# Recurrence and top-4 mixture of experts on one core: no dummy matmuls between the recurrence's steps, b2 as one rounded pass over stacked gates, gate transposes behind the down product

## The reference

```python
# x: (32 sequences, 32 steps, 128), h0 = cond: (32, 128)
xw = x @ Wx + b
h[t] = tanh(xw[:, t] + h[t-1] @ Wh)            # 32 steps, one after the other
# mixture of experts over the 1024 tokens h, 16 experts, 4 chosen
xn = h * rsqrt(mean(h * h) + 1e-5) * norm_scale
vals, idx = top_k(xn @ wg + bg, 4)
gate_full = one_hot(idx) @ softmax(vals)       # (1024, 16)
hh = xn @ w1[e] + b1[e]                        # 128 -> 2 x 128, for every expert
a, b = min(hh[::2], 7), clip(hh[1::2], -7, 7)
s = a * sigmoid(1.702 * a) * (b + 1)
y = s @ w2[e] + b2[e]
out = x + h + sum over e of gate_full[:, e] * y[e]
```

## Time and profile before

| | |
|---|---|
| three runs | 109.14, 109.22, 110.36 us; median 109.22 |
| profiled execution | 110.22 us, span of its instructions 108.4 us |
| PE busy | 102.9 us (95%), 562 matmuls |
| weight loads busy | 87.0 us (80%) |
| DVE, ACT, POOL busy | 64.6 (60%), 60.8 (56%), 63.8 us (59%) |
| chain that ended last, by engine | PE 79%, DVE 9%, ACT 5%, DMA 2% |

### The profile page before, as it was taken

One profiled execution on the slowest core, in us unless ns is written; L12 is line 12 of the kernel. 1 busy time (PEld: TensorE's weight loads), 2 busy tenths in 40 slices (PEclk: granted clock), 3 DMA queues, 4 the chain that ended last, 5 costly groups with the idle time before them and its releaser, 6 DMA issues.

```text
span 108.4 us, 1718 instructions
## 1 busy us (share of the span) xinstructions
PE 102.9 (95%) x562; PEld 87.0 (80%) x562; DVE 64.6 (60%) x173; ACT 60.8 (56%) x139; POOL 63.8 (59%) x76
## 2 busy tenths in 40 slices
PE   7899999999999999999999969999999999999980
PEld 2557689988899999999989958886888888888760
DVE  0101367876818976399747996578266656666730
ACT  5144826899646486767716645665364566645400
POOL 3004348987791996449980799896444466545400
PEclk9999999999999999999999999999999999999999
DMA  2997930007930002991058814991000000000012
GB/s 77 235 335 266 398 113 0 0 6 234 390 159 3 0 0 74 296 379 39 12 165 246 308 60 116 336 361 59 6 0 0 0 3 0 0 0 0 0 48 48
DMA packets 4936, 12.94 MB, mean 119 GB/s; under 512 B 752, under 2 KB 1728, under 8 KB 4928
## 3 DMA queue, kind: packets, MB, share of 16 engines
q1 hardware_dynamic: 4704, 12.67, 34.7%
q10 hardware_dynamic: 224, 0.17, 0.6%
HBM read 12.25 MB, written 0.59 MB: 118 GB/s over the span
## 4 chain that ended last, share of the span: by engine, by line
PE 79%; DVE 9%; ACT 5%; DMA 2%; issue 1%; DVEq 0%
PE psA L774 19%; PE psB L774 17%; PE psY L804 10%; PE psR L804 5%; PE psR L722 5%; PE psM L804 5%; PE psY L722 2%; DMA wx_x_sb<-in_wx_x 2%; PE psA L751 2%; PE psM L729 2%; PE psR L714 2%; ACT psA L483 2%; PE psR L816 2%; ACT psA L492 2%; PE psM L816 2%; DVE lin L667 1%
## 5 line engine op out<-in xcount | busy, mean ns | idle before, releaser
L406 POOL TENSOR_TENSOR actg<-act,gate_cols 128x512 f32<-128x512 f32 x31 | 39.4, 1279 | 13.7 <-DVE act L682 12.9
L667 DVE TENSOR_SCALAR lin<-psB,one_b1b 128x256 f32<-128x256 f32 (+1 forms) x48 | 26.0, 569 | 23.3 <-PE psB L774 23.3
L483 ACT ACTIVATE psA<-psA,lim_b1a 128x256 f32<-128x256 f32 (+1 forms) x48 | 23.8, 515 | 26.5 <-PE psA L774 26.5
L682 DVE SCALAR_TENSOR_TENSOR act<-lin,psA 128x512 f32<-128x512 f32 x32 | 21.9, 686 | 1.8 <-ACT psA L492 0.5
L492 ACT ACTIVATE psA<-psA,limit_col 128x512 f32<-128x512 f32 x32 | 21.1, 660 | 0.8
L774 PE MATMUL psA<-xn_hi,w_hi 128*128 128x256 f32 (+1 forms) x48 | 20.5, 428 | 0.0
L804 PE MATMUL psY<-actg,w_sb 128*128 128x256 f32 x64 | 17.1, 389 | 0.0
L774 PE MATMUL psB<-xn_hi,w_hi 128*128 128x256 f32 (+1 forms) x48 | 16.0, 332 | 0.0
L774 PE MATMUL psA<-xn_hi,w_lo 128*128 128x256 f32 (+1 forms) x48 | 15.8, 328 | 0.0
L774 PE MATMUL psB<-xn_lo,w_hi 128*128 128x256 f32 (+1 forms) x48 | 15.6, 325 | 0.0
L774 PE MATMUL psB<-xn_hi,w_lo 128*128 128x256 f32 (+1 forms) x48 | 15.5, 323 | 0.0
(11 more groups left out here) (82 smaller groups left out, 136.0 us busy)
## 6 DMA issues: line engine op xcount, KB each, us to landing
gate_cols<-gate_rows SPq DMA_DIRECT2D x16, 512.0 KB, 6.0
w_sb<-in_w SPq DMA_DIRECT2D x4, 512.0 KB, 8.0
w_sb<-in_w SPq DMA_DIRECT2D x4, 256.0 KB, 9.3
out<-yT SPq DMA_DIRECT2D x3, 128.0 KB, 1.7
wx_x_sb<-in_wx_x SPq DMA_DIRECT2D x1, 320.0 KB, 6.0
wx_x_sb<-in_wx_x SPq DMA_DIRECT2D x2, 128.0 KB, 2.5
small_h<-in_small ACTq DMA_DIRECT2D x1, 105.0 KB, 2.7
gate_rows<-gT SPq DMA_DIRECT2D x4, 16.0 KB, 1.4
```

Of the source, the lines that this page charges most:

```text
L406: nc.gpsimd.tensor_tensor(by_pair(actg[:, u % SUM_DEPTH, w]), by_pair(act[:, u % ACT_DEPTH, w]), gate_block(u, w), ALU.mult).then_inc(actg ...
L483: last = nc.scalar.activation(psA[u % 2][:, o], psA[u % 2][:, o], ACT.Relu, scale=-1.0, bias=lim_b1a[:, e0 + k:e0 + k + 1])
L667: last = nc.vector.tensor_scalar(lin[:, v % 2, o], psB[v % 2][:, o], one_b1b[:, e0 + k:e0 + k + 1], LIMIT + 1.0, ALU.add, ALU.min)
L682: nc.vector.scalar_tensor_tensor(act[:, v % ACT_DEPTH, 0:w], lin[:, v % 2, 0:w], 1.0 - LIMIT, psA[v % 2][:, 0:w], ALU.max, ALU.mult).then_ ...
```

## The change

1. PE's head: the ten dummy matmuls between steps and the one behind them are gone. The raw logits of tile 0 come after step 6, those of tile 1 behind the sums of tile 1; `x_wx(3, 2)` becomes `x_wx(3, 1)` ahead of `lay_rstd(1)` and `x_wx(4, 1)` behind it.
2. b2 comes three times stacked (48 x 128). DVE rounds it to fp32r and replaces the third copy by what rounding left (`b2_parts`, at v = 1). The gates are laid out as [rounded, rest, rounded, zeros, exact], 80 columns (`gates_split`, two more DVE instructions a pair, and one more POOL memset at the start), so one rounded product with 48 rows adds high x high, low x high and high x low. The transposes are 80 x 128; ACT copies the exact part (gT) and then the stacked part (gS, fp32r). `down` waits for gS.
3. From v = 4 on the transposes stand behind `down(v - 4)`.
4. The last chunk's accumulators are 384 and 128 columns wide (psR, psM) in place of 256 and 256; the last product waits for both of DVE's pieces, and the last addition and store are 128 columns wide.

```diff
@@ gates_scale
-                nc.vector.tensor_tensor(
+                mark(nc.vector.tensor_tensor(
                     gates[:, ts, :], gate_sum[:, ts, :],
                     inv[:, ts].rearrange("p (j o) -> p j o", o=1).to_broadcast([P, 2, E]),
-                    ALU.mult).then_inc(scale_done, 1)
+                    ALU.mult))
+
+            def gates_split(q):
+
+                settled()
+                ts = slice(2 * q, 2 * q + 2)
+                high = gates_w[:, ts, 0:4 * E].rearrange("p j (a b e) -> p j a b e", a=2, b=2)[:, :, :, 0, :]
+                mark(nc.vector.tensor_copy(high.bitcast(F32R), gates[:, ts, :].rearrange("p j (a e) -> p j a e", a=1)
+                                           .to_broadcast([P, 2, 2, E])))
+                settled()
+                nc.vector.tensor_tensor(gates_w[:, ts, E:2 * E], gates[:, ts, :], gates_w[:, ts, 0:E],
+                                        ALU.subtract).then_inc(scale_done, 1)
@@ copy_gates
-                nc.scalar.activation(gT[:, q * PW:(q + 1) * PW], psX[0:E, 0:PW], ACT.Copy).then_inc(gT_ready, 1)
+                qc = slice(q * PW, (q + 1) * PW)
+                nc.scalar.activation(gT[:, qc], psX[4 * E:5 * E, 0:PW], ACT.Copy).then_inc(gT_ready, 1)
+                nc.scalar.activation(gS[:, qc], psX[0:3 * E, 0:PW], ACT.Copy).then_inc(gS_ready, 1)
@@ vector
+            def b2_parts():
+
+                dve.wait_ge(b2_loaded, 16)
+                mark(nc.vector.tensor_copy(b2_w[:, :], b2_sb[:, :]))
+                settled()
+                low = slice(2 * E, 3 * E)
+                nc.vector.tensor_tensor(b2_w[low, :], b2_sb[low, :], b2_w[low, :].bitcast(F32),
+                                        ALU.subtract).then_inc(b2_ready, 1)
@@ transpose_gates
-                    last = nc.tensor.transpose(psX[0:E, k * P:(k + 1) * P], gates[:, j, :], ident[:, :])
+                    last = nc.tensor.transpose(psX[0:5 * E, k * P:(k + 1) * P], gates_w[:, j, :], ident[:, :])
@@ down
-                    pe.wait_ge(gT_ready, first_pair(c + 1))
+                    pe.wait_ge(gS_ready, first_pair(c + 1))
                     for o, y in y_parts(c):
-                        nc.tensor.matmul(y, b2_sb[:, :], gT[:, cols(c)][:, o], start=True, stop=False)
+                        nc.tensor.matmul(y, b2_w[:, :], gS[:, cols(c)][:, o], start=True, stop=False)
@@ head of the tensor program
                 step(t)
-                if t in (0, 1, 2, TL, TL + 2):
-                    keep_warm(2)
-                elif t == 3:
+                if t == 3:
                     x_wx(1, 1)
                 elif t == TL + 1:
                     pe.wait_ge(consts_ready, 1)
                     sums(0).then_inc(m_mm, 1)
-                else:
+                elif t == TL + 2:
+                    pe.wait_ge(wg_ready, 1)
+                    raw_logits(range(0, 1), psB[0])
+                elif t == HEAD - 1:
                     lay_rstd(0)
                     x_wx(2, 1)
-            keep_warm(1)
+            sums(1).then_inc(m_mm, 1)
+            raw_logits(range(1, 2), psB[0]).then_inc(raw_mm, 1)
             pe.wait_ge(step_done, HEAD)
-            sums(1).then_inc(m_mm, 1)
-            pe.wait_ge(wg_ready, 1)
-            raw_logits(pair_tiles(0), psB[0]).then_inc(raw_mm, 1)
+            x_wx(3, 1)
             lay_rstd(1)
-            x_wx(3, 2)
+            x_wx(4, 1, start=False)
@@ loop over the units
-                for q in at(GATES_T, v):
-                    transpose_gates(q)
+                if v < LAG:
+                    for q in at(GATES_T, v):
+                        transpose_gates(q)
                 for q in at(STATS, v):
                     sums(pair_group(q))
                     raw_logits(pair_tiles(q), psM).then_inc(m_mm, 1)
                 if v >= LAG:
                     down(v - LAG)
+                    for q in at(GATES_T, v):
+                        transpose_gates(q)
@@ the last chunk
-                return [(slice(k * PW, (k + 1) * PW), y_end_bank(k)[:, 0:PW]) for k in range(2)]
+                return [y_end(k) for k in range(2)]
@@ down_half
-                    pe.wait_ge(actg_tail, k + 1)
+                    pe.wait_ge(actg_tail, 2)
```

More of the change, by code:

```diff
@@ L92, in adaln_rnn_moe_kernel @@
         bg_sb = sb("bg_sb", [P, E])
-        b2_sb = sb("b2_sb", [E, H])
+        b2_sb = sb("b2_sb", [3 * E, H])
+        b2_w = sb("b2_w", [3 * E, H], F32R)
         w1_sb = sb("w1_sb", [H, E, 2, I])
@@ L128, in adaln_rnn_moe_kernel @@
         gate_sum = sb("gate_sum", [P, NT, E])
-        gates = sb("gates", [P, NT, E])
-        gT = sb("gT", [E, NT * P])
+        gates_w = sb("gates_w", [P, NT, 5 * E])
+        gates = gates_w[:, :, 4 * E:5 * E]
+        gT_all = sb("gT_all", [5 * E, NT * P])
+        gT = gT_all[4 * E:5 * E, :]
+        gS = sb("gS", [3 * E, NT * P], F32R)
         gate_rows = nc.dram_tensor("gate_rows", [NQ, E, PW], F32)
@@ L176, in adaln_rnn_moe_kernel @@
         gT_ready = sem("gT_ready")
+        gS_ready = sem("gS_ready")
+        b2_ready = sem("b2_ready")
         a_mm = sem("a_mm")
@@ L179, in adaln_rnn_moe_kernel @@
         y_mm = sem("y_mm")
-        y_end = sem("y_end")
+        y_done = sem("y_done")
         relu_done = sem("relu_done")
@@ L235, in pieces, with y_end @@
             return [slice(0, h), slice(h, W)] if u == NU - 1 else [slice(0, width(u))]
-        def y_end_bank(k):
-            return psM if k else psR
+        def y_end(k):
+            o = [slice(0, 3 * P), slice(3 * P, W)][k]
+            return o, (psM if k else psR)[:, 0:o.stop - o.start]
         def gate_block(u, o):
@@ L328, in _ @@
             for k in range(2):
-                o = slice((NT - 4 + 2 * k) * P, (NT - 2 + 2 * k) * P)
+                o = slice((NT - 1) * P if k else (NT - 4) * P, NT * P if k else (NT - 1) * P)
                 sp.wait_ge(yT_ready, NC + k)
@@ L351, in _ @@
             nc.gpsimd.memset(expo[:, :, 0:1], 1.0)
+            nc.gpsimd.memset(gates_w[:, :, 3 * E:4 * E], 0.0)
             nc.gpsimd.iota(iota_e[:, :], pattern=[[1, E]], base=0, channel_multiplier=0,
@@ L503, in _ @@
             acte.wait_ge(yT_ready, NC + 1)
-            store(acte, slice((NT - 2) * P, NT * P), slice(P // 2, P))
+            store(acte, slice((NT - 1) * P, NT * P), slice(P // 2, P))
         @block.vector
@@ L617, in close_gates @@
                 gates_scale(q)
+                gates_split(q)
+            def b2_parts():
[5 more added lines that the diff above has]
+                                        ALU.subtract).then_inc(b2_ready, 1)
             def w1_low(p):
@@ L683, in _ @@
                                                    psA[v % 2][:, 0:w], ALU.max, ALU.mult).then_inc(act_done, 1)
+                if v == 1:
+                    b2_parts()
                 for q in at(RSTD, v):
@@ L698, in _ @@
             for k in range(2):
[L699 to L702, removed]
+                dve.wait_ge(y_done, k + 1)
+                o, y = y_end(k)
+                o = slice((NT - 4) * P + o.start, (NT - 4) * P + o.stop)
+                nc.vector.tensor_tensor(yT[:, o], xT[:, o], y, ALU.add).then_inc(yT_ready, 1)
         @block.tensor
@@ L709, in turn, with x_wx @@
                     pe.wait_ge(m_read, psM_turn(what) - 1)
-            def x_wx(j, n):
+            def x_wx(j, n, start=True):
                 pe.wait_ge(x_loaded if j > 2 else x1_loaded if j else wx_x0_loaded, 16)
-                nc.tensor.matmul(xw_cols(j, n), wx_sb, xT[:, j * P:(j + n) * P], start=True, stop=True,
+                nc.tensor.matmul(xw_cols(j, n), wx_sb, xT[:, j * P:(j + n) * P], start=start, stop=True,
                                  skip_group_check=True)
@@ L732, in raw_logits @@
             def raw_logits(ts, bank):
-                for k, j in enumerate(ts):
+                for j in ts:
+                    k = j % 2
                     last = nc.tensor.matmul(bank[:, 16 + k * E:16 + (k + 1) * E], hT[:, N + j * P:N + (j + 1) * P],
@@ L788, in down @@
                     if c == 0:
-                        pe.wait_ge(b2_loaded, 16)
+                        pe.wait_ge(b2_ready, 1)
                     elif c < NC - 1:
@@ L810, in down_half @@
                 c, e0, r = unit(u)
-                o = slice(k * PW, (k + 1) * PW)
+                o, y = y_end(k)
                 if u < NU - 1:
@@ L814, in down_half @@
                 else:
-                    pe.wait_ge(actg_tail, k + 1)
-                ins = nc.tensor.matmul(y_end_bank(k)[:, 0:PW], w2_sb[:, e0, :], actg[:, u % SUM_DEPTH, o],
+                    pe.wait_ge(actg_tail, 2)
+                ins = nc.tensor.matmul(y, w2_sb[:, e0, :], actg[:, u % SUM_DEPTH, o],
                                        start=False, stop=(u == NU - 1))
                 if u == NU - 1:
-                    ins.then_inc(y_end, 1)
+                    ins.then_inc(y_done, 1)
             keep_warm(WARM_START, WARM)
@@ L901 @@
         "w2": f["ffn_w2"].transpose(1, 0, 2),
```

(2 more changed lines are left out.)

2 lines of the change are left out of this document (1 added, 1 removed).

## The result

| | before | after |
|---|---|---|
| median, executions on the same chips | 109.79 us (4; 109.14 to 113.00) | 112.85 us (4; 112.68 to 113.42) |
| ratio | | 1.031, 95% interval 1.022 to 1.040 |
| profiled execution, span | 110.22, 108.4 us | 112.70, 110.9 us |
| first `up(0,0)` matmul at | 15.22 | 15.07 |
| first `down(0)` matmul | 29.40 | 29.27 |

Some executions of these kernels are slower by a per cent or more, whatever the change; the medians count them and the ratios leave them out (before, 113.00).

A forecast was written before the change was run, and what follows sets the result against it. Bounds: recurrence to 12 us, then DVE/POOL statistics, PE at low clock, ACT to 26, then PE except two routing chains. Terms sum to a 1.55 us gain, 107.7 us from the median; own range 107.2 to 108.3, with rivals 106.8 to 109.2.

The forecast's parts named there:

- the price of the split: Two more dependent DVE instructions ahead of act(10): 0.4 to 0.7 us together, so up(12,0) ready at 51.7 to 52.05.
- Dummies lengthen no step, price 0: Head's recurrence: the dummy matmuls finish before tanh releases the next step, so removing them changes nothing: 0 us.
- Head's order, 0.1: Ahead of up(0,0): raw logits and x_wx moved into waits; gain 0.1 us, bounds 0 and 0.35.
- gS and b2 at v=4, 0.15: At down(0): shorter b2 nearly all spent on the second ACT copy and actg(0); gain 0.15 us, from -0.27 to 0.35.
- b2 at v=12, 0.4: One rounded pass replaces the four-cycle fp32 b2 product at v=12; gain 0.4 us, bounds 0.3 to 0.5.
- At v=20, 0.7: Two b2 products of 1.05 us together become about 0.35 us; gain 0.7 us, bounds 0.55 to 0.8.
- Transposes behind the down, nothing at v=15: down(11), put first, waits for actg(11) to the same moment: gain 0, or loss up to 0.3 us if act(14) is later.
- 384 and 128, a loss of 0.15: Last chunk's units: 128-column passes barely cover a weight load; loss 0.15 us, bounds 0 to 0.4.
- The end, 0.3: Kernel's tail: no wait ahead of the last product, narrower last addition; gain 0.3 us, bounds 0.1 to 0.6.
- The best case: All terms' bounds at their best: a gain of 2.9 us, giving 106.3 us.
- Rival (b): DVE's split becomes the bound at v=11 and v=15, ACT copy uncovered at v=4: 0.9 us more, 108.6; chance 0.17.
- Rival (a): Clock rises later because PE has gaps before 15 us: 108.8 us one unit later, 109.9 two; chance 0.2.

The follow-up runs named there:

- the run with POOL held, dummies and old head: Changed kernel with GpSimd waiting for the finished gates before xn_low at v=6, 10, 14, and the head as before: 110.77 us, ratio 1.013 to before.
- b2 alone: Kernel before with only stacked gates, their split, rounded b2 and the second ACT copy; dummies kept: 115.88 us, ratio 1.056.
- the old order: Changed kernel with the transposes ahead of the down product again, split and all else as changed: 115.44 us, ratio 1.048 to the kernel before.
- two added subtractions: Kernel before with two more dependent two-input DVE subtractions behind each set of gates, results unread, transposes waiting for the second: 116.96 us, ratio 1.067.

## Why the prediction was wrong

The step that failed is the price of the split, and the rule behind it. For v=10 the prediction said: such steps are 0.20 apart, while gates itself took 0.36, so 0.4 to 0.7 for the two. They took 0.65 + 1.18 and the gaps, 1.9 us. Its terms were a gain of 0.05 at v=10 (bounds +0.15 and -0.3) and 0 at v=14 (down to -0.3); measured, they were losses of 1.26 and 1.71. The pair made at v=6 was in no term at all, so it stood at nothing without a reason, and it cost 0.96: at v=7 nothing waited before, and 1.9 us were more than PE's slack. Together 3.9 us, which is more than all gains, and the sign followed. A sign that the prediction had named came too: PE waits 0.27 for act ahead of `up(16,0)`, where 0.2 was the limit.

The evidence stood in its own rows. In the earlier trace rows gates takes 0.36 from 50.37 and ends at 50.73; in the earlier trace rows POOL's product ends at 49.38 + 1.30 = 50.68. At v=14 the same: POOL's product ends at 63.13, and the transposes, released by gates, start at 63.23. The 0.36 was read as the upper end of a duration. It was a wait for POOL's end, and what it said of the next instruction is not "0.36 again" but "until POOL's next one is over": 0.73 for xn_low, 1.28 for a product. The Trainium skill states it (SBUF — State Buffer, section "Who interferes with whom"): DVE and GpSimd share a port pair, held for a whole instruction, and a DVE instruction with two SBUF inputs contends with a GpSimd instruction that reads SBUF, while `tensor_reduce` on this chip and one with a single SBUF input outside the two-port modes do not. The traces agree on three kinds: subtraction 1.18, reduction 0.19, subtraction with a PSUM input 0.42 throughout. The cast has a single SBUF input, and the section counts casts among what can enter a two-port mode; its 0.65 beside POOL fits, but no row shows in which mode it ran. `hot` in the last section does not fit the rule. The prediction didn't draw on it.

Point by point:
- *Dummies lengthen no step, price 0*: right as a median (0.999), and the steps are 1.02 apart in both traces, but for one (next point). That the head runs at the low level was wrong for some executions.
- *Head's order, 0.1*: `up(0,0)` starts 0.15 earlier, and that is luck. The step at 8.04 stands at 7.88 already, ahead of all that was reordered; from there to `up(0,0)` it is 7.18 and 7.19 us. In the trace of before ACT's cast of w_hi waited for its load and pushed the tanh back:

```profile
7.39 0.42 ACT L449 ACTIVATE w_hi<-w_sb 128x256 fp32r<-128x256 f32 x1 [0.58 <-DMA w_sb<-in_w]
7.71 0.27 ACT L441 ACTIVATE small_h<-psY,small_h 128x32 f32<-128x32 f32 x1
```

  In the changed kernel the cast ran from 6.91. The old head can do the same: in the run with POOL held, dummies and old head the step is at 7.88 and `up(0,0)` at 15.07. The order gained nothing that the traces show.
- *gS and b2 at v=4, 0.15*: `down(0)` at 29.27 instead of 29.40. These 0.13 are the same head start; from `up(0,0)` on it is 14.18 and 14.20, so this term was nothing. The split at v=0 was not hidden as claimed either: DVE took 0.62 and 0.66 there, and PE waited 1.04 for act(0) at 22.00. ACT's pace took that up.
- *b2 at v=12, 0.4*: 0.31. *At v=20, 0.7*: 0.63. Right within a tenth.
- *Transposes behind the down, nothing at v=15*: wrong for the changed kernel; once DVE is late, the order is worth about 2 us. For the kernel before, no run tries it alone.
- *384 and 128, a loss of 0.15*: units are 2.25 us in both. No loss.
- *The end, 0.3*: 0.27 behind the last matmul, 0.1 ahead of it. Right in the trace; as a ratio of its own (0.997) it is not clear of 1.
- *The best case*: the upper bounds add up to a gain of 2.75, not 2.9; this changes nothing.
- *Rival (b)*, the split as the bound, had place and mechanism but a price of 0.9 us at most. Its chance of 0.17 was not the fault so much as its size: nothing in the sum could grow beyond 0.3.
- *Rival (a)*, the clock, was looked for in the head. It did come as a mechanism, in three traces (b2 alone, the old order, two added subtractions), behind a pause that DVE had made, and not in that of the changed kernel.

## What to carry to other kernels

When a small DVE instruction has two durations in one trace, look which POOL row ends where the longer one ends. If it is always the same, the longer duration is a wait, and each further dependent instruction of that kind costs up to a whole POOL instruction. Put an input in PSUM, use an operation that doesn't wait (here a reduction), hold POOL for the moment, or give the work to ACT; and keep work for PE that lies across the wait, since a pause can take the clock as well. Then price the instruction at every place where it stands, also where nothing waits yet: 1.9 us used up the slack of v=7.

## What the runs showed of the hardware

- A dependent DVE instruction with two SBUF inputs, or an SBUF to SBUF cast, ran until 0.05 us behind the end of the POOL instruction beside it (three of three at v=10 above), and so took 0.65 or 1.18 us in place of 0.19. Reductions (0.19 in the run that adds them, 0.15 to 0.28 in the others) and the reciprocal (0.17) didn't wait.
- Not every POOL instruction has this effect. `hot` on DVE, two inputs in SBUF, ran for its usual 0.29 us inside POOL's power (changed kernel, timeline):

```profile
48.43 1.32 POOL L376 TENSOR_TENSOR expo<-euler,diff 128x6 f32<-128x6 f32 x1 [2.92 <-DVE diff L587]
...
48.89 0.29 DVE L600 TENSOR_TENSOR hot<-iota_e,top_f 128x128 f32<-128x128 f32 x1
```

  By the rule of the Trainium skill cited above it would wait, since both read SBUF; here the measurement decides. The same at 17.05 us: two subtractions `w_lo` of 128x256, both inputs in SBUF, take 0.76 together, the first of them wholly inside POOL's power (16.37 to 17.70). Why the power leaves room (few elements, much computation) was not tried.
- Behind pauses of 2.73 and 2.74 us without a matmul TensorE came back at the low level for some 3 us in two traces, and behind one of 1.94 us in a third; behind the 2.73 us of that third trace it did not, nor behind 1.94 and 1.93 us in the first two. Behind three pauses of 0.3 to 0.8 us with a down between them it did not.
- The granted clock of the profile can read 1.00 while the matmuls run at the low level; in the three traces where it had risen and fallen it reads 0.50 behind the fall. The spacing of like matmuls is the safer reading.
